# Router worked by halves of the image rows, its vector instructions moved between steps, Newton steps split, round loop written out

## The chip, the cores and the metric

One core of one Trainium2 chip runs the kernel. The metric is the device time of one execution in microseconds; a lower time is better. The engines are named as in the profile: PE is TensorE's matmul, PEld its weight load, DVE is VectorE, ACT ScalarE, POOL GpSimd, SP SyncE (here the only queue that issues DMAs).

## The reference

The input is x[16, 64, 112, 112] in float32. Two blocks are added to it in turn.

```
x = x + conv_ref(ln_c(x))          # ln_c: over the 64 channels of a pixel, eps 1e-6
    pooled = [max over channels, mean over channels]
    conv_ref(v) = v * sigmoid(conv3x3(pooled) + conv_b)
t = tokens of x                    # a token is a pixel, 64 channels
t = t + moe(ln_t(t))               # ln_t: over the channels, eps 1e-5
    router_probs = softmax(v @ router_w + router_b)       # 8 experts
    top 2, their probabilities divided by their sum
    moe(v) = sum over the two of p_k * (v @ expert_w[k] + expert_b[k])
```

## The kernel before

Two images form a pair (`PAIRS` = 8), eight image rows of a pair form a step (`ROWS` = 8, `STEPS` = 14 steps in a pair). Three phases are laid over each other, one pair apart. In round r, phase A reads pair r: PE centres the channels and forms raw router logits (`centre_rows`, L440), ACT copies them out (`centred_to_sbuf`, L877 and L881) and squares them with a running sum (`square`, L896, or `square_group`, L907), and DVE takes the channel maximum (`channel_max`, L639). Phase B of pair r-1 is the router, once a round on tiles of 112 x 224 tokens (all rows of both images): two reciprocal square roots by Newton steps, the 3x3 convolution (`convolve`, L541), its sigmoid, the affine factors, and the choice of the two best experts with ties broken by a priority (`key`, `half_key`, `quarter_key`, `key_max`). Phase C of pair r-2 computes the experts in units: step v has six units for DVE (`scale_unit`, L662: gate from PSUM times x) and two for POOL (L1105, after ACT has copied the gate out, L939). PE spreads the gates (`spread`, L462), multiplies the scaled tokens by the expert weights (`experts`, L517) and adds the biases (`biases`, L511). The eight spreads of a step go through two PSUM slots; one is free again when the unit that read it is done.

The gates come to PE in three bf16 parts made by ACT and POOL (L918, L1113 `rest_one`, L924, L1119 `part_three`), which PE transposes (`turn`, L455) and ACT copies to `s` (`turned_to_sbuf`, L931). The transposes and `centre_rows` write the same PSUM pair `tm`, so that `centre_rows` waits for that copy.

Each engine works through a list written out by hand, the same in each step except for what the router adds. On PE: spread of DVE unit 1 and POOL unit 1, the last experts of v-1, biases, experts 0, `turn`, spreads 2 and 3, `centre_rows` 0, experts 1 and POOL 0, spread 4 and POOL 0 of v+1, (the convolution,) experts 2, `spread_a1`, biases, experts 3, spread 5 and spread 0 of v+1, `centre_rows` 1, experts 4 and POOL 1. DVE: unit 1, `gate(r, step, False)`, the second `finish` of v-1, units 2 and 3, `channel_max`, unit 4, `gate(r, step, True)`, `finish`, unit 5, unit 0 of v+1, `channel_max`. The prediction calls the router's two places in DVE's step the head place and the middle place. POOL: unit 1, `rest_one`, router work, unit 0 of v+1, `scale_x` (L1130), `part_three`.

The router's DVE work before: the whole first square root (11 instructions, L699 to L709) in the middle place of step 0, the second with `rho` in that of step 2; `pooled` in the head of step 1, the affine factors in the head of step 2 (L734 to L741); then one or two instructions in each place, those on `key` with all 224 columns in steps 5, 6, 10 and 11.

Rounds 0 and 1 have no phase C. In round 0 POOL does all squares, after its own setup; ACT may not overwrite a tile before it is squared. Rounds 3 to 7 are a hardware loop (`Fori`) on each engine, with wait counts in registers; the others are written out.

Of the kernel before, what the change touches and what calls it, by code (L numbers as in the profile page):

```python
# [28 lines left out]
ALU = mybir.AluOpType  # L29
# [19 lines left out]
EARLY = 5  # L49
JOIN = 5  # L50
# [14 lines left out]
B_DVE = ("i1", "p1", "t10", "u10", "r10", "t11", "u11", "r11", "t12", "u12", "r1", "pool_max", "pool_mean", "av", "am", "part_sum", "v2", "i2", "p2", "t20", "u20", "r20", "t21", "u21", "r21", "t22", "u22", "r2", "rho",  # L65
         "top_0", "ge_0", "top_1", "ge_1", "key", "half", "quarter", "key_max", "oh1", "dl_0", "dl_1",
         "top2_0", "top2_1", "d", "ge2_0", "ge2_1", "key2", "half2", "quarter2", "key_max2", "oh2")
B_NORM = ("e1", "e2")
GUESS = 0x5F3759DF
B_POOL = ("lg_0", "bias_0", "lg_1", "bias_1", "m1_0", "m1_1", "m2_0", "qb_0", "qg_0", "m2_1", "qb_1", "qg_1")  # L70
B_ACT = ("sig", "wide", "qa_0", "g1", "g2", "wide2", "qa_1")
# [35 lines left out]
def gated_expert_program(nc, x, conv_w, conv_b, router_w, router_b, expert_w, expert_b, const_f, const_g, out):  # L107
# [3 lines left out]
    with ExitStack() as ctx:  # L111
# [131 lines left out]
        def at(r, first, per, n):  # L243
            return (r - first) * per + n if isinstance(r, int) else r * per + (n - first * per)

        def due(count):

            return not isinstance(count, int) or count > 0

        def a_at(r, per_step, step, n):  # L250

            if isinstance(r, int) and r >= PAIRS:
                return PAIRS * STEPS * per_step
# [11 lines left out]
        def on(r, v):  # L265

            return not isinstance(r, int) or 0 <= (r - 2) * STEPS + v < PAIRS * STEPS
# [4 lines left out]
        def squared_at(r, step, n):  # L272

            if isinstance(r, int) and r >= PAIRS:
                return (PAIRS - 1) * STEPS * QUADS
            return at(r, 1, QUADS * STEPS, QUADS * step + n)

        def summed_at(r, step, g):
            if r == 0:
                return NGRP * step + g + 1  # L280
            return NGRP * STEPS + step + 1 + (step // 2 if g == 0 and step % 2 == 0 else (step + 1) // 2 if g == 0 else step // 2 + 1)
# [5 lines left out]
        def centre_pairs(r):  # L287

            early = [moe, gb[:, 0:2, :], gb[:, 2:4, :], tm]
            return [tm] if not isinstance(r, int) or r >= 2 else early[0:4 - r]  # L290
# [34 lines left out]
        prios = prio[:, :].unsqueeze(1).to_broadcast([W, 2 * H, E])  # L325
# [4 lines left out]
        def _(sp):  # L330
# [41 lines left out]
            def body(r, A, steps=STEPS):  # L372
                pairs = [r - n if isinstance(r, int) else sp.snap(r - n) for n in range(4)]
                lead = XA - 1 if isinstance(r, int) and r < 2 else 2
# [907 lines left out]
```

## Time and profile before

| | us |
|---|---|
| median of 3 runs | 1703.19 |
| lowest and highest | 1702.29, 1706.99 |
| profiled execution, its own time | 1706.22 |
| its span, first to last instruction | 1704.4 |

| engine | busy us | share of the span |
|---|---|---|
| PE | 1460.7 | 86% |
| DVE | 1345.4 | 79% |
| POOL | 1142.8 | 67% |
| ACT | 1060.3 | 62% |

The profile is of one execution. The shares are means over a start without phase C (the first 145 us), six rounds with all phases or nearly so, and two rounds without phase A at the end. The granted TensorE clock has a mean of 0.94 of full speed.

### The profile page before, as it was taken

What the parts mean: (1) busy time and instruction counts of PE and PEld (TensorE: products, weight loads), DVE (VectorE), ACT (ScalarE), POOL (GpSimd) and SP (SyncE); (2) the same over time, 40 slices, a digit from 0 to 9 for tenths busy, and PEclk for the clock granted to TensorE, in tenths of its full rate; (3) what the DMA queues carried; (4) which work ended last, traced back from release to release, by engine and by line L of the source; (5) the groups of instructions that cost most, each with busy time, mean ns of one, the idle gap of its engine ahead of it and who ended that gap; (6) DMA issues with size and microseconds to landing.
All of it is one profiled execution on the core that took longest, in us unless ns stands there. A gap on an engine that the chain in (4) does not pass through costs nothing.

```text
span 1704.4 us, 37629 instructions
## 1 busy us (share of the span) xinstructions
PE 1460.7 (86%) x12198; PEld 685.1 (40%) x12198; DVE 1345.4 (79%) x1575; ACT 1060.3 (62%) x4015; POOL 1142.8 (67%) x743
## 2 busy tenths in 40 slices
PE   6865899869997799977999779988799788989999
PEld 5763344434443344433444334433344333323333
DVE  3796888788887788878887788868888778977776
ACT  2566677747776577756777558775678624434442
POOL 6335667848676576855768566775667758788775
PEclk9956899989999999999999899999999989999999
DMA  5441465536555455544655445553555444555554
GB/s 173 120 136 39 120 185 173 174 109 184 176 162 154 141 163 172 164 154 127 183 178 168 126 142 173 175 184 121 151 175 154 129 128 136 171 144 172 174 174 127
DMA packets 85883, 260.40 MB, mean 153 GB/s; under 512 B 13744, under 2 KB 13744, under 8 KB 85680
## 3 DMA queue, kind: packets, MB, share of 16 engines
q1 hardware_dynamic: 85680, 257.85, 50.6%
q8 instruction: 109, 1.79, 0.4%
q14 instruction: 94, 0.77, 0.2%
HBM read 206.41 MB, written 51.38 MB: 151 GB/s over the span
## 4 chain that ended last, share of the span: by engine, by line
PE 54%; DVE 18%; issue 9%; ACT 9%; POOL 1%; DVEq 1%; ACTq 0%; POOLq 0%
PE moe L517 31%; PE gb L462 8%; DVE gx L662 8%; PE tm L440 6%; PE moe L511 4%; ACT s L931 3%; DVE u L704 2%; ACT sq L896 2%; PE tm L501 2%; PE tm L455 2%; DVE quarter_key L771 2%; DVE p L701 2%; DVE u L706 1%; PE tm L541 1%; ACT ge L982 1%
## 5 line engine op out<-in xcount | busy, mean ns | idle before, releaser
L662 DVE TENSOR_TENSOR gx<-gb,xd 128x896 f32<-128x896 f32 x672 | 710.5, 1085 | 205.1 <-PE gb L462 192.2
L517 PE MATMUL moe<-gx,wc 128*64 128x448 f32 x3584 | 841.7, 570 | 1.2 <-POOL parts L1119 1.1
L1105 POOL TENSOR_TENSOR gx<-gs,xd 128x896 f32<-128x896 f32 x224 | 519.0, 2317 | 452.3 <-ACT gs L939 423.6
L939 ACT ACTIVATE gs<-gb 128x896 f32<-128x896 f32 x224 | 204.9, 915 | 302.3 <-PE gb L462 301.7
L462 PE MATMUL gb<-s,cg 54*128 54x448 bf16 x1792 | 273.2, 365 | 118.6 <-DVE gx L662 104.9
L896 ACT ACTIVATE sq<-xct 112x64 f32<-112x64 f32 x1400 | 337.8, 243 | 24.6 <-DVE early_s L649 6.4
L517 PEld LDWEIGHTS moe<-gx,wc 128*64 128x64 f32 x3584 | 221.3, 139 | 247.3 <-issue 190.4
L896 ACT ACTIVATION_READ_ACCUMULATOR sq<-xct 112x1 f32 x1400 | 263.1, 188 | 0.0
L1130 POOL TENSOR_TENSOR tt<-xc,a1s 128x896 f32<-128x896 f32 x112 | 235.2, 2100 | 18.7 <-ACT a1s L946 16.0
L440 PE MATMUL tm<-rhs,xa 64*112 64x74 f32 x2800 | 176.7, 267 | 69.4 <-ACT s L931 63.1
L462 PEld LDWEIGHTS gb<-s,cg 54*128 54x128 bf16 x1792 | 61.1, 95 | 398.9 <-DVE gx L662 229.6
L440 PEld LDWEIGHTS tm<-rhs,xa 64*112 64x112 f32 x2800 | 168.0, 182 | 112.1 <-issue 100.6
L877 ACT ACTIVATE xct<-tm 112x512 f32<-112x512 f32 x175 | 103.9, 594 | 107.9 <-PE tm L440 103.6
L675 DVE TENSOR_TENSOR ot<-moe,tt 128x448 f32<-128x448 f32 x224 | 138.4, 618 | 35.7 <-PE moe L517 35.5
L931 ACT ACTIVATE s<-tm 128x896 bf16<-128x896 bf16 x112 | 102.3, 914 | 80.1 <-PE tm L455 79.8
L946 ACT ACTIVATE a1s<-tm,ones 128x896 f32<-128x896 f32 x112 | 112.8, 1007 | 46.3 <-PE tm L501 46.3
L639 DVE TENSOR_REDUCE stats<-xct 112x8 f32<-112x512 f32 x144 | 97.9, 680 | 41.9 <-ACT logit_mean L881 41.5
L455 PEld LDWEIGHTS tm<-cg,parts 112*64 112x64 bf16 x1792 | 63.8, 115 | 64.0 <-issue 61.4
L1113 POOL TENSOR_TENSOR res<-q,parts 112x288 f32<-112x288 f32 x112 | 87.6, 782 | 0.3 <-ACT parts L918 0.3
L511 PE MATMUL moe<-s,bh 118*64 118x448 bf16 x448 | 84.4, 370 | 0.0
L511 PE MATMUL moe<-s,bl 118*64 118x448 bf16 x448 | 84.1, 369 | 0.0
L1119 POOL TENSOR_TENSOR parts<-res,parts 112x288 bf16<-112x288 f32 x112 | 82.5, 737 | 0.0
(97 smaller groups left out, 1342.5 us busy)
## 6 DMA issues: line engine op xcount, KB each, us to landing
xd<-in_x_dram SPq DMA_DIRECT2D x448, 224.0 KB, 3.9
xa<-in_x_dram SPq DMA_DIRECT2D x112, 448.0 KB, 4.2
xc<-in_x_dram SPq DMA_DIRECT2D x112, 448.0 KB, 4.4
out_dram<-ot SPq DMA_DIRECT2D x112, 448.0 KB, 3.0
gx<-in_const_g_dram SPq DMA_DIRECT2D x1, 384.0 KB, 4.7
cf<-in_const_f_dram SPq DMA_DIRECT2D x1, 332.5 KB, 2.7
gx<-in_L_ffn_expert_w_dram SPq DMA_DIRECT2D x1, 128.0 KB, 4.5
cf<-in_L_ffn_expert_b_dram SPq DMA_DIRECT2D x6, 2.0 KB
```

What stands on the lines that cost most here:

```text
L440: last = pe.matmul(pair[:, b, j, :], xa[chans, step % XA, row * W:(row + 1) * W], rhs1[chans, :], start=True, stop=True)
L462: last = pe.matmul(gb[:, 2 * slot + b, 0:HALF], cg[rows, k * P:(k + 1) * P], s[rows, v % 2, c * HALF:(c + 1) * HALF], start=True, stop=True)
L511: pe.matmul(moe[b * CH:(b + 1) * CH, c, 0:HALF], w[:, b * CH:(b + 1) * CH], s[0:SR, v % 2, c * HALF:(c + 1) * HALF], start=(n == 0), stop= ...
L517: last = pe.matmul(moe[b * CH:(b + 1) * CH, c, 0:HALF], wc[:, k * CH:(k + 1) * CH], gx[:, u, b, :], start=False, stop=(k == KT - 1), skip_ ...
L662: dve.tensor_tensor(gx[:, i, :, :], gb[:, 2 * slot:2 * slot + 2, 0:HALF], xd[:, v % 2, :, c * HALF:(c + 1) * HALF], ALU.mult).then_inc(sca ...
L675: dve.tensor_tensor(ot[:, sl, cols], moe[:, c, 0:HALF], tt[:, sl, cols], ALU.add).then_inc(final, 1)
L896: last = act.activation(sq[:, n, :], xct[:, step % 2, n, :], ACT.Square, accum_out=to[:, 1, lo + n:lo + n + 1])
L931: act.activation(s[:, v % 2, :], turn_out[:, 0:TOK], ACT.Copy).then_inc(s_ready, 1)
L939: act.activation(gs[:, j, :, :], gb[:, 2:4, 0:HALF], ACT.Copy).then_inc(gate_out, 1)
L946: act.activation(a1s[:, v % 2, :].rearrange("p (c t) -> p c t", c=2), tm[:, :, 0:HALF], ACT.Identity, bias=ones[:, :], scale=1.0).then_inc ...
L1105: pool.tensor_tensor(gx[:, ND + j, :, :], gs[:, j, :, :], xd[:, v % 2, :, j * HALF:(j + 1) * HALF], ALU.mult).then_inc(scaled_p, 1)
L1130: pool.tensor_tensor(tt[:, sl, :], xc[:, sl, :], a1s[:, sl, :], ALU.mult).then_inc(scaled_x, 1)
```

## The change

- The router's 224 columns are worked in two halves (`first`, `second`, 112 columns each), one after the other: `half_router(r, h, place)` does eight places for one half. A place is half a step, `place = 2 * step + late`. Half 0 has places 12 to 19, half 1 places 20 to 27. ACT's and POOL's router operations are split and shifted in the same way.
- A Newton root is split: `root_guess` and the first Newton step in one place, the second and the third in the next two. The initial guess is one instruction in place of two.
- On DVE `gate(r, step, False)` stands before unit 1 (was after it), `gate(r, step, True)` before unit 4 (was after it).
- On PE `turn` stands before the biases and experts 0 (was after them); the convolution moves from step 1 to step 2. On ACT `turned_to_sbuf` stands before the last squares of the step before (was after them).
- In round 0, ACT does the squares of the first seven steps (`ACT_STEPS`), POOL those of the others.
- `EARLY` and `JOIN` (how many steps' statistics go to the side tiles, and when they are joined) are 6, were 5.
- Rounds 3 to 7 are written out, with constant wait counts.

```diff
-EARLY = 5
-JOIN = 5
+EARLY = 6
+JOIN = 6
+ACT_STEPS = 7
...
-            with pe.Fori(3, PAIRS) as r:
+            for r in range(3, PAIRS):
                 body(r, True, True)
...
                     if on(r, v - 1):
                         experts_of_dve(r, v - 1, 5)
+                    if ahead:
+                        turn(r, step, v + 1)
                     if cur:
                         biases(r, v, 0)
-                    if ahead:
-                        turn_ready(r, step, v + 1)
-                    if cur:
                         experts_of_dve(r, v, 0)
-                    if ahead:
-                        turn(v + 1)
...
-                    if Bp and step == 1:
+                    if Bp and step == 2:
                         convolve(r, A)
...
+            def largest_key(r, h, again, rows):
+
+                own(r, f"ge{again}_{h}")
+                dve.tensor_tensor(key[:, rows, :], ge[:, rows, :], prios, ALU.mult).then_inc(b_dve, 1)
+                own(r, f"key{again}_{h}")
+                dve.tensor_tensor(half_key[:, rows, :], key[:, rows, 0:4], key[:, rows, 4:8], ALU.max).then_inc(b_dve, 1)
+                own(r, f"half{again}_{h}")
+                dve.tensor_tensor(quarter_key[:, rows, :], half_key[:, rows, 0:2], half_key[:, rows, 2:4], ALU.max) \
+                   .then_inc(b_dve, 1)
+                own(r, f"quarter{again}_{h}")
+                dve.tensor_tensor(key_max[:, rows], quarter_key[:, rows, 0], quarter_key[:, rows, 1], ALU.max) \
+                   .then_inc(b_dve, 1)
...
+            def half_router(r, h, place):
+
+                rows = (first, second)[h]
+                if place == 0:
+                    b_done(dve, r, B_POOL, f"bias_{h}")
+                    largest(top, lg, rows).then_inc(b_dve, 1)
+                elif place == 1:
+                    own(r, f"top_{h}")
+                    at_top(lg, top, rows).then_inc(b_dve, 1)
+                elif place == 2:
+                    largest_key(r, h, "", rows)
+                elif place == 3:
+                    first_expert(r, h)
+                elif place == 4:
+                    second_logit(r, h)
+                elif place == 5:
+                    own(r, f"top2_{h}")
+                    at_top(dl, top2, rows).then_inc(b_dve, 1)
+                elif place == 6:
+                    largest_key(r, h, "2", rows)
+                else:
+                    second_expert(r, h)
...
+                dve.tensor_scalar(p_int, e_int, -0.5, float(GUESS), ALU.mult, ALU.add).then_inc(b_dve, 1)
...
             def gate(r, step, late):
 
...
+                place = 2 * step + late
+                if place == 1:
+                    root_guess(r, 1)
+                    root_step(r, 1, 0, p)
+                elif place == 2:
+                    root_step(r, 1, 1, p)
+                elif place == 3:
+                    root_step(r, 1, 2, r1)
+                elif place == 4:
+                    to_pool(r)
+                elif place == 6:
+                    affine(r)
+                elif place == 7:
+                    root_guess(r, 2)
+                    root_step(r, 2, 0, p)
+                elif place == 8:
+                    root_step(r, 2, 1, p)
+                elif place == 9:
+                    root_step(r, 2, 2, r2)
+                    scale(r)
+                elif 12 <= place < 20:
+                    half_router(r, 0, place - 12)
+                elif place >= 20:
+                    half_router(r, 1, place - 20)
...
-                    if cur:
-                        scale_unit(r, v, 1)
                     if Bp:
                         gate(r, step, False)
+                    if cur:
+                        scale_unit(r, v, 1)
...
-                    if cur:
-                        scale_unit(r, v, 4)
                     if Bp:
                         gate(r, step, True)
                     if cur:
+                        scale_unit(r, v, 4)
                         finish(r, v, 0)
...
                     if parting:
                         part_one(r, v + 2)
+                    if ahead:
+                        turned_to_sbuf(r, v + 1)
+                    if Bp:
+                        router(r, step)
                     if A and step > 0:
                         square(r, step - 1, 3)
...
-            for step in range(STEPS):
+            for step in range(ACT_STEPS, STEPS):
                 for g in range(NGRP):
                     square_group(step, g)
```

POOL's router after: step 0 the first `e` (and the second gates of the round before), step 3 the second `e`, step 5 logits and bias of half 0, steps 6 and 7 those of half 1, steps 9 to 12 the gates of half 0, step 13 and steps 0 to 2 of the next round those of half 1. On ACT `widen` (the widened `key_max`) stands in steps 7, 9, 11 and 13, the sigmoids of the gap in steps 8 and 12.

## Rows read from the trace of the kernel before

**Rows 1.** Windows by round: us, busy (x) of PE, PEld, DVE, ACT, POOL; PEclk, DMA.

```profile
145.70:1369.40 1223.70, 1055.06 (x9074) 482.81 (x9076) 995.45 (x1144) 852.86 (x3548) 830.60 (x505) 0.95 0.52 155
1369.40:1545.20 175.80, 157.53 (x1078) 56.92 (x1080) 141.81 (x149) 66.83 (x92) 133.19 (x82) 0.95 0.50 143
1545.20:1683.40 138.20, 135.78 (x990) 49.58 (x988) 98.90 (x104) 57.16 (x77) 100.39 (x67) 1.00 0.59 174
```

**Rows 2.** Windows: the same columns, steps 1 to 4, 13 and the next 0.

```profile
752.80:771.06 18.26, 17.12 (x121) 8.41 (x122) 12.65 (x14) 10.02 (x41) 9.54 (x6) 0.83 0.43 128
771.06:791.05 19.99, 12.16 (x112) 5.54 (x110) 19.15 (x26) 10.27 (x46) 8.79 (x6) 0.97 0.38 115
791.05:806.56 15.51, 14.37 (x108) 6.15 (x109) 11.03 (x13) 9.54 (x40) 10.68 (x6) 0.82 0.50 152
806.56:819.11 12.55, 11.86 (x110) 5.46 (x109) 10.11 (x12) 9.90 (x44) 11.51 (x8) 1.00 0.62 182
...
924.16:938.86 14.70, 11.93 (x110) 5.42 (x109) 8.90 (x11) 10.26 (x46) 12.36 (x9) 1.00 0.77 240
938.86:958.86 20.00, 13.60 (x109) 6.32 (x110) 15.12 (x20) 10.23 (x43) 10.31 (x7) 0.87 0.34 104
```

**Rows 3.** Timeline of DVE, step 0: start, us, instruction (first root's beginning).

```profile
743.05 2.17 DVE L701 TENSOR_SCALAR p<-p 112x224 int32<-112x224 int32 x1
...
748.27 0.39 DVE L709 SCALAR_TENSOR_TENSOR p<-u,p 112x224 f32<-112x224 f32 x1
```

**Rows 4.** Timeline of POOL beside it.

```profile
742.99 2.09 POOL L1105 TENSOR_TENSOR gx<-gs,xd 128x896 f32<-128x896 f32 x1 [1.40 <-ACT gs L939]
```

**Rows 5.** Timeline of PE: after the burst, and at the convolution.

```profile
752.80 0.56 PE L462 MATMUL gb<-s,cg 54*128 54x448 bf16 x2 [5.70 <-DVE gx L662]
...
763.29 2.52 PE L541 MATMUL tm<-pooled,band 112*112 112x224 f32 x12
```

**Rows 6.** PE, step 13 (head 924.16): biases, turn, spread 2, centring, loop edge; a wait.

```profile
925.44 0.36 PE L511 MATMUL moe<-s,bh 118*64 118x448 bf16 x2
...
926.58 0.57 PE L455 MATMUL tm<-cg,parts 112*64 112x112 bf16 x16
927.08 0.55 PE L462 MATMUL gb<-s,cg 54*128 54x448 bf16 x4
928.33 1.01 PE L440 MATMUL tm<-rhs,xa 64*112 64x74 f32 x16 [0.69 <-ACT s L931]
...
938.86 0.56 PE L462 MATMUL gb<-s,cg 54*128 54x448 bf16 x4 [2.08 <-issue]
...
PE tm L440 <- ACT s L931: 63.1, 82, 1.3
```

**Rows 7.** Timeline of POOL, step 4 (its PE head is at 806.56).

```profile
806.56 0.71 POOL L1119 TENSOR_TENSOR parts<-res,parts 112x288 bf16<-112x288 f32 x1
808.23 2.87 POOL L1105 TENSOR_TENSOR gx<-gs,xd 128x896 f32<-128x896 f32 x1 [0.96 <-ACT gs L939]
```

**Rows 8.** The page's costliest groups: a DVE unit (busy, mean ns, idle before).

```profile
L662 DVE TENSOR_TENSOR gx<-gb,xd 128x896 f32<-128x896 f32 x672 | 710.5, 1085 | 205.1 <-PE gb L462 192.2
```

**Rows 9.** Timeline of DVE: key instructions beside POOL (833), without POOL (104); affine without POOL.

```profile
833.96 2.16 DVE L771 TENSOR_TENSOR quarter_key<-half_key 112x448 bf16<-112x448 bf16 x1
...
104.07 0.61 DVE L769 TENSOR_TENSOR half_key<-key 112x896 bf16<-112x896 bf16 x1
104.72 0.39 DVE L771 TENSOR_TENSOR quarter_key<-half_key 112x448 bf16<-112x448 bf16 x1
...
81.57 0.55 DVE L737 TENSOR_TENSOR avm<-avm,logit_mean 112x224 f32<-112x224 f32 x1
```

**Rows 10.** Start of the kernel: ACT's wait in round 0, first copy of round 1, PE's pace.

```profile
29.48 0.60 ACT L877 ACTIVATE xct<-moe 112x512 f32<-112x512 f32 x1 [16.08 <-POOL sq L1094]
...
62.10 0.60 ACT L877 ACTIVATE xct<-moe 112x512 f32<-112x512 f32 x1 [0.85 <-PE moe L440]
...
14.52 3.19 PE L440 MATMUL gb<-rhs,xa 64*112 64x74 f32 x32
```

More of the change, by code:

```diff
@@ L243, in at @@
         def at(r, first, per, n):
-            return (r - first) * per + n if isinstance(r, int) else r * per + (n - first * per)
+            return (r - first) * per + n
         def due(count):
-            return not isinstance(count, int) or count > 0
+            return count > 0
         def a_at(r, per_step, step, n):
-            if isinstance(r, int) and r >= PAIRS:
+            if r >= PAIRS:
                 return PAIRS * STEPS * per_step
@@ L372, in body @@
             def body(r, A, steps=STEPS):
-                pairs = [r - n if isinstance(r, int) else sp.snap(r - n) for n in range(4)]
-                lead = XA - 1 if isinstance(r, int) and r < 2 else 2
+                pairs = [r - n for n in range(4)]
+                lead = XA - 1 if r < 2 else 2
                 for step in range(steps):
@@ L432, in centre_rows @@
                         pe.wait_ge(a1_out, count)
-                if step == 1 and g == 1 and (not isinstance(r, int) or r >= 2):
+                if step == 2 and g == 1 and r >= 2:
                     b_done(pe, r, B_ACT, "sig")
@@ L614, in _ @@
             body(2, True, True)
-            with pe.Fori(3, PAIRS) as r:
+            for r in range(3, PAIRS):
                 body(r, True, True)
@@ L849, in _ @@
             early_body(0, False)
-            dve.wait_ge(setup_pool, POOL_SETUP)
             early_body(1, True)
             body(2, True, True)
-            with dve.Fori(3, PAIRS) as r:
+            for r in range(3, PAIRS):
                 body(r, True, True)
@@ L871, in centred_to_sbuf @@
                             act.wait_ge(joined, count)
-                    if step == EARLY and (not isinstance(r, int) or r > 0):
-                        b_done(act, r, B_POOL, "lg_1")
+                    if step in (EARLY, STEPS // 2) and r > 0:
+                        b_done(act, r, B_POOL, "lg_0" if step == EARLY else "lg_1")
                 if due(count := a_at(r, NGRP, step, g + 1)):
@@ L976, in affine_to_q, with widen, gates, router @@
                    .then_inc(b_act, 1)
[L978 to L982 removed]
+            def widen(r, h, again):
+                rows = (first, second)[h]
+                b_done(act, r, B_DVE, f"key_max{again}_{h}")
+                act.activation(ge[:, rows, :], wide(key_max, rows), ACT.Copy).then_inc(b_act, 1)
+            def gates(r, h):
+                rows = (first, second)[h]
+                b_done(act, r, B_DVE, f"d_{h}")
+                act.activation(g1[:, rows], gap[:, rows], ACT.Sigmoid, scale=-1.0).then_inc(b_act, 1)
+                act.activation(g2[:, rows], gap[:, rows], ACT.Sigmoid, scale=1.0).then_inc(b_act, 1)
+            def router(r, step):
+                if step == 7:
+                    widen(r, 0, "")
                 elif step == 8:
[L984 removed]
+                    gates(r, 0)
                 elif step == 9:
[L986 to L988 removed]
+                    widen(r, 0, "2")
+                elif step == 11:
+                    widen(r, 1, "")
+                elif step == 12:
+                    gates(r, 1)
+                elif step == 13:
+                    widen(r, 1, "2")
             def early_body(r, Bp):
@@ L1052, in _ @@
             body(2, True, True)
-            with act.Fori(3, PAIRS) as r:
+            for r in range(3, PAIRS):
                 body(r, True, True)
@@ L1253, in _ @@
             body(2, True)
-            with pool.Fori(3, PAIRS) as r:
+            for r in range(3, PAIRS):
                 body(r, True)
```

336 lines of the change are left out of this document (145 added, 191 removed).

## The prediction

> **What bounds the kernel now.** I read the windows first, by round and by step, then the timelines of the dearest steps.
>
> From the first copy of `s` (145.7) six rounds take 1223.7 us, 204.0 each; then a round without phase A takes 175.8, and 13 steps of the last 138.2, or 10.63 a step [rows 1]. Phase A and the router together separate a step of 10.63 from a mean step of 14.6. Step 4 has only two small router instructions and takes 12.55, with PE busy for 11.86 of it at full clock [rows 2]. Fourteen of those are 175.7, so the router costs 28 us a round. Steps 1, 2, 3, 13 and 0 hold nearly all of it: 18.26, 19.99, 15.51, 14.70 and 20.00 [rows 2].
>
> In step 0 DVE starts the root in its middle place. The second instruction takes 2.17, because POOL's unit started 0.06 us earlier: both end near 745.1 [rows 3, 4]. A longer DVE instruction of the same root takes 0.39 [rows 3]. PE, waiting for DVE's unit 5, idles 5.70 us and then continues at half clock: 1.2 GHz shows in the mean clock of 0.83 in step 1 and 0.82 in step 3 [rows 2, 5]. So a burst costs three times: its length, the block by POOL, and the half clock after it.
>
> In ordinary steps PE is the bound with one hole: `centre_rows` waits 0.69 for ACT's `s`, 63.1 us over 82 steps [rows 6].
>
> **Turn earlier.** PE does the first biases and four expert matmuls after `turn` instead of before: `turn` takes the place of the biases at 925.44, 1.1 earlier [rows 6]. The 0.69 hole goes in the steps where nothing else is late. ACT copies `s` before its squares, so it is ready for it. Needed for this is POOL's `part_three`, which ends 0.71 after the head of step 4 [rows 7]; the turn now starts 2.42 after the head and would start 1.3 after it. A step becomes 12.55 - 0.70 = 11.85. The bounds of the gain are 0 (POOL's chain, late by 0.7 in steps with much router work, takes the hole's place) and 63 us. I take 0.70 in steps with phase A. Without phase A there is no such hole, and `part_three` sits later; I charge 0.2 a step there.
>
> **Bursts split.** Nine Newton instructions in a burst become three in a place, about 1.25 us at 0.39 and a gap [rows 3], and two instructions fall away. What a place can hold: in the head place DVE starts at 0.71 (POOL's `part_three` holds it until then), POOL's unit starts at 1.67 [rows 7], and unit 1 must be over when PE wants spread 2, 2.92 after the head (927.08 less 924.16, rows of the turn) [rows 6]. With 1.09 for the unit [rows 8] the head place holds 1.1 us. It also must have *started* its last instruction by 1.67, or it waits for POOL's unit until 3.8. In the middle place, before unit 4, POOL is idle for some 1.7 us, and that is about what fits.
>
> By this, place by place for one round:
> - Newton steps in heads and middles: 0 to 0.2 each. They start at 0.71, 1.13 and 1.55. Cover: PE's experts, turn and biases.
> - Step 0, middle: guess and Newton step wait for POOL's `e`, which follows second gates on POOL. The third instruction meets POOL's unit: +2.4 (between 0, if ahead of it, and 4.2, if two are caught).
> - `pooled`: 0.38 + 0.60, ends at 1.7: 0. The row for the affine multiply without POOL is 0.55 [rows 9]; affine is four instructions of 0.38 to 0.55, and its third would start at 1.70, 0.03 after POOL's unit. I take the block: unit 1 starts at 4.7 in place of 1.75, +2.9 (between 0.2 and 2.9).
> - Four key places, all in heads: multiply 0.61 (half of 1792 columns; 896 take 0.61), half 0.39, quarter and maximum about 0.27 [rows 9]. They start at 0.71, 1.35, 1.77: the quarter is caught, as the full one is now (2.16 against 0.39 alone) [rows 9]. Unit 1 starts at 4.4, PE's spread 2 is 2.5 late: 4 x 2.5 = 10.0 (between 4 x 0.3 and 10.0; the upper end, since a start at 1.77 is after 1.67).
> - Reductions and comparisons with one logit tile (1.1 each), `first_expert` 1.7, ACT's `widen` halves and POOL's operations: they fit their places; lateness of `part_three` and POOL's two operations in step 5, 1.5 together.
> - Convolution: 2.5 on PE as now, only a step later [rows 5].
>
> **The lock, by the notes.** The rows show who starts first: DVE begins beside POOL and waits, or POOL's unit lasts 2.87 when a DVE instruction is in flight [rows 7]. The Trainium skill, SBUF — State Buffer, Who interferes with whom, says that a DVE instruction with two SBUF inputs and a GpSimd instruction that reads SBUF exclude each other for a whole instruction, and that a reduction is exempt. The trace agrees (2.17 and 2.87). That rule speaks against this change: smaller instructions give more starts at which DVE can lose. By it the four key places come to 10 us a round; by a mere sharing of bandwidth they would come to about 1.
>
> **Half clock.** Six places of 2.4 us or more idle PE. Now the loop edge idles it 2.08 [rows 6], and the step after it has a mean clock of 0.87, with the root's idle in it [rows 2]. The pieces of a clock fall are 3.4 us long in the record, so one costs 1.7. I take three a round: 5.1 (0 to 10).
>
> **Rounds written out.** PE waits 2.08 at the loop edge for instructions [rows 6]; four edges, some 8 to 12 us with the clock, go. They are in the 204.0 and not in my base. Written-out rounds already show no such wait.
>
> **Sum of a round.** 14 x 11.85 = 165.9; convolution 2.5; step 0 2.4; affine 2.9; keys 10.0; small 1.5; clock 5.1: 190.3. Less 2.3, because in four steps the 2.5 us idle hides the small items and part of a clock fall: 188. Six rounds: 6 x (204.0 - 188) = 96 us gained. The round without phase A: 148.8 + 2.5 + 2.9 + 10 + 3.4 + 2.8 = 170.4, 5 gained. The last: 13 x 0.2 = 2.6 lost.
>
> **Round 0.** ACT waits 16.08 us for POOL's squares behind its setup [rows 10]. With squares on ACT, the pace is PE's 3.19 for 32 matmuls, 2.99 a step: round 1 starts at 9.5 + 14 x 2.99 = 51.4 in place of 62.1 [rows 10]. ACT and DVE need less for a step. Gain 11 (8 to 12). POOL's setup is over by step 7. Round 1 I leave as it is: DVE's work is a chain with the same instructions, and what the split saves in the burst comes back in the ACT and DVE waits for each other (-6 to +6).
>
> 1704.4 - 96 - 5 + 3 - 11 = 1595 for the span; the profiled run is 1.8 longer than its span, and the median is 3.0 below the profiled run: 1594, say 1595.
>
> **Rivals.**
> - A, the places fit: the keys and the affine factors are not caught, since POOL's unit starts a little later behind a gate copy that waits for its turn on ACT. Then 10 + 2.9 + 3.4 go from each of seven rounds, 16 x 7 = 114: 1480. For it: the two starts are 0.03 and 0.1 us too late only. Against: the gate copy follows the head's spread, which the change leaves alone.
> - B, the turn only changes what it waits for (`part_three`): 0.7 x 84 = 59 comes back: 1654. For it: a unit lengthened to 2.87 [rows 7] puts `part_three` 0.8 later, at 1.5, and the turn is wanted at 1.3.
> - C, slower: each root, key and one-hot place starts after POOL's unit, because ready signals arrive late in a moving schedule. Eight more heads and middles at 2.5, and six more clock falls of 1.7: 30 a round, seven rounds 210: 1805. It decides from some 4.6 further caught places a round on (109 gained / 7 rounds / 3.4 each). Against: Newton steps start at 0.71.
> - D, no change: the router's DVE work only moves and DVE's total is the bound. DVE is busy for 995 of 1224 us, its waits for POOL included [rows 1], 81%, and a round 8% shorter still holds that. About 1700.
>
> **Chances.** Forecast 0.52, A 0.22, B 0.20, C 0.03, D 0.03. The range runs from A to B: 1475 to 1660; C and D and what lies beyond both ends are left out. A measurement of this kernel can tell 0.3% from no change. Faster 0.94, same 0.02, slower 0.04.
>
> **What would show it.** Steps 4, 5, 8 and 10 at 11.9 with no wait of `centre_rows` for `s`: the turn. Quarter and maximum of about 2 us in half the key places, unit 1 late by 2.5: the lock; at 0.3 each, rival A. No PE wait above 4 us after the start. ACT's first copy of round 1 near 51. A wait of the transposes for `part_three` in most steps is B.

## The result and the profile after

| | before | after |
|---|---|---|
| median of 4 runs, us | 1704.61 | 1584.64 |
| lowest and highest | 1702.29, 1706.99 | 1582.87, 1590.98 |
| profiled execution | 1706.22 | 1582.87 |
| its span | 1704.4 | 1581.1 |
| PE, DVE, POOL, ACT busy | 86, 79, 67, 62% | 91, 84, 68, 69% |

The ratio after to before is 0.930, 95% interval 0.927 to 0.933: 120 us faster.

The windows of the kernel after, by round (they answer to [rows 1]) and then for three steps: step 0, the ordinary step 4, and a step with a key place ([rows 2]). Columns: us, busy (x) of PE, PEld, DVE, ACT, POOL; PEclk, DMA share, GB/s.

```profile
137.60:1246.60 1109.00, 1028.29 (x9066) 477.35 (x9068) 965.47 (x1190) 866.01 (x3579) 778.10 (x504) 0.95 0.57 171
1246.60:1420.40 173.80, 154.62 (x1081) 52.96 (x1077) 149.34 (x165) 67.63 (x96) 131.27 (x84) 0.97 0.51 146
1420.40:1558.90 138.50, 135.96 (x991) 46.76 (x988) 98.96 (x105) 57.22 (x77) 102.33 (x68) 1.00 0.59 174
674.87:688.73 13.86, 11.67 (x110) 5.39 (x109) 11.76 (x15) 10.24 (x45) 10.73 (x9) 1.00 0.52 166
726.00:737.60 11.60, 11.60 (x111) 5.37 (x110) 11.41 (x18) 9.92 (x44) 7.64 (x6) 1.00 0.68 200
788.29:804.17 15.88, 13.30 (x110) 5.94 (x108) 13.37 (x16) 10.98 (x46) 9.34 (x8) 0.89 0.50 146
```

The span became 123.3 us shorter. The first copy of `s` comes 8.1 earlier (145.7 to 137.6). The six rounds behind it are 114.7 shorter (1223.7 to 1109.0). The round without phase A is 2.0 shorter, the last 13 steps are 0.3 longer, and what follows them is 1.2 longer.

A round in the middle takes 184.3. Measured between the starts of spread 1, eight of its 14 steps take 11.60 to 11.80; the second window from the end is one of them, with PE busy throughout. The others are step 0 with 13.86, step 2 with 14.06 (11.60 and the convolution's 2.46), and four key steps (7, 9, 11 and 13, whose head place works on `key`) with 15.69 to 15.88.

The last row is the finding: this key step is 4.28 longer than an ordinary one, PE idles for 2.58 of it, and the mean granted clock is 0.89. The four of a round add 16.9. DVE's timeline there, then POOL's and PE's (start, us, instruction, idle time before it):

```profile
788.40 1.05 DVE L692 TENSOR_TENSOR key<-ge,prio 112x896 bf16<-112x896 bf16 x1
789.49 0.39 DVE L694 TENSOR_TENSOR half_key<-key 112x448 bf16<-112x448 bf16 x1
789.92 2.17 DVE L696 TENSOR_TENSOR quarter_key<-half_key 112x224 bf16<-112x224 bf16 x1
792.13 0.67 DVE L699 TENSOR_TENSOR key_max<-quarter_key 112x112 bf16<-112x112 bf16 x1
792.72 1.08 DVE L665 TENSOR_TENSOR gx<-gb,xd 128x896 f32<-128x896 f32 x1
```

```profile
788.27 0.71 POOL L1171 TENSOR_TENSOR parts<-res,parts 112x288 bf16<-112x288 f32 x1
789.88 2.08 POOL L1157 TENSOR_TENSOR gx<-gs,xd 128x896 f32<-128x896 f32 x1 [0.91 <-ACT gs L972]
791.92 0.75 POOL L1165 TENSOR_TENSOR res<-q,parts 112x288 f32<-112x288 f32 x1
```

```profile
793.86 0.55 PE L468 MATMUL gb<-s,cg 54*128 54x448 bf16 x4 [2.58 <-DVE gx L665]
...
795.42 3.03 PE L523 MATMUL moe<-gx,wc 128*64 128x448 f32 x8
```

The quarter maximum starts 0.04 after POOL's unit and lasts 2.17, until POOL's unit is over. The last maximum starts 0.21 after POOL's next operation and takes 0.67, until that one is over. Unit 1 follows at 792.72, 4.43 after the head (788.29), and PE waits for it.

Steps 11 and 13 look the same, with starts 0.03 to 0.04 after POOL's unit. In step 7 POOL's unit starts later (at 763.10, 2.10 after the head), the quarter comes before it and takes 0.27, and the last maximum is the one that is held:

```profile
763.15 2.16 DVE L699 TENSOR_TENSOR key_max<-quarter_key 112x112 bf16<-112x112 bf16 x1
```

The waits of PE and of its weight load, grouped (in total, times, longest). PE's wait for `s` of [rows 6], 63.1 us, is down to 1.3; what PE waits for now are DVE's units. The 37 times are the 28 key places of seven rounds (2.31 to 2.58 each), step 0 with 2.19 to 2.21 in five rounds, and four at the turn to the rounds without phase A:

```profile
PE gb L468 <- DVE gx L665: 91.0, 37, 4.4
...
PE tm L461 <- POOL parts L1171: 3.4, 6, 1.7
...
PEld tm L461 <- POOL parts L1171: 41.4, 97, 2.5
```

### The profile page after: what moved, and what is told of

It is laid out like the page before. It is cut to its first block, busy times and chain, and to the rows that moved or that the text cites. A ratio compares the mean times of both kernels' runs of the same rounds, so it can differ in the third digit from the quotient of the medians.

```text
span 1581.1 us, 34381 instructions
## 1 busy us (share of the span) xinstructions
PE 1432.2 (91%) x12198; PEld 673.0 (43%) x12198; DVE 1326.6 (84%) x1647; ACT 1084.0 (69%) x4061; POOL 1072.8 (68%) x729
## 4 chain that ended last, share of the span: by engine, by line
PE 66%; DVE 16%; issue 8%; ACT 2%; POOL 1%; DVEq 0%; ACTq 0%; POOLq 0%
PE moe L523 36%; PE gb L468 12%; DVE gx L665 8%; PE tm L447 7%; PE moe L517 4%; DVE quarter_key L696 3%; PE tm L507 3%; PE tm L461 2%; DVE key L692 2%; PE tm L547 1%; DVE stats L642 1%; DVE half_key L694 1%; ACT sq L928 1%; ACT logit_mean L994 0%; DVE u L762 0%
## 5 line engine op out<-in xcount | busy, mean ns | idle before, releaser
L1157 POOL TENSOR_TENSOR gx<-gs,xd 128x896 f32<-128x896 f32 x224 | 470.5, 2100 | 400.8 <-ACT gs L972 395.7
L468 PE MATMUL gb<-s,cg 54*128 54x448 bf16 x1792 | 260.3, 359 | 97.0 <-DVE gx L665 91.0
L523 PEld LDWEIGHTS moe<-gx,wc 128*64 128x64 f32 x3584 | 224.8, 140 | 256.2 <-issue 203.6
L1182 POOL TENSOR_TENSOR tt<-xc,a1s 128x896 f32<-128x896 f32 x112 | 236.3, 2110 | 12.5 <-issue 10.7
L468 PEld LDWEIGHTS gb<-s,cg 54*128 54x128 bf16 x1792 | 56.6, 94 | 439.9 <-DVE gx L665 330.4
L447 PEld LDWEIGHTS tm<-rhs,xa 64*112 64x112 f32 x2800 | 182.2, 192 | 29.6 <-issue 11.0
L447 PE MATMUL tm<-rhs,xa 64*112 64x74 f32 x2800 | 180.1, 273 | 11.1 <-ACT logit_mean L913 8.3
L642 DVE TENSOR_REDUCE stats<-xct 112x8 f32<-112x512 f32 x128 | 87.0, 680 | 22.7 <-ACT logit_mean L913 21.6
L1165 POOL TENSOR_TENSOR res<-q,parts 112x288 f32<-112x288 f32 x112 | 81.7, 730 | 9.6 <-ACT parts L951 9.6
L461 PEld LDWEIGHTS tm<-cg,parts 112*64 112x64 bf16 x1792 | 57.2, 111 | 65.4 <-POOL parts L1171 41.4
L517 PE MATMUL moe<-s,bh 118*64 118x448 bf16 x448 | 80.8, 354 | 0.0
L517 PE MATMUL moe<-s,bl 118*64 118x448 bf16 x448 | 80.5, 352 | 0.0
```

What stands on the lines that cost most here:

```text
L447: last = pe.matmul(pair[:, b, j, :], xa[chans, step % XA, row * W:(row + 1) * W], rhs1[chans, :], start=True, stop=True)
L468: last = pe.matmul(gb[:, 2 * slot + b, 0:HALF], cg[rows, k * P:(k + 1) * P], s[rows, v % 2, c * HALF:(c + 1) * HALF], start=True, stop=True)
L517: pe.matmul(moe[b * CH:(b + 1) * CH, c, 0:HALF], w[:, b * CH:(b + 1) * CH], s[0:SR, v % 2, c * HALF:(c + 1) * HALF], start=(n == 0), stop= ...
L523: last = pe.matmul(moe[b * CH:(b + 1) * CH, c, 0:HALF], wc[:, k * CH:(k + 1) * CH], gx[:, u, b, :], start=False, stop=(k == KT - 1), skip_ ...
L1157: pool.tensor_tensor(gx[:, ND + j, :, :], gs[:, j, :, :], xd[:, v % 2, :, j * HALF:(j + 1) * HALF], ALU.mult).then_inc(scaled_p, 1)
L1182: pool.tensor_tensor(tt[:, sl, :], xc[:, sl, :], a1s[:, sl, :], ALU.mult).then_inc(scaled_x, 1)
```

## The experiments

Each kernel is the kernel after with the edit shown, unless it says otherwise. Medians are of 4 runs. "To before" is the ratio to the kernel before on the same chip, with its 95% interval. The kernel before took 1703.75, 1704.33 and 1705.51 in the three groups of runs, so a difference between two groups is uncertain by some 2 us from that alone.

### The key multiply in the place before

```diff
                     at_top(lg, top, rows).then_inc(b_dve, 1)
+                    key_of(r, h, "", rows)      # the same for "2"; largest_key begins with half_key
```

> The changed kernel with one DVE instruction moved: the multiply that makes key goes to the middle place before, behind the comparison (1.08 + 0.61 us there), so that the head place has only half, quarter and maximum, started at about 0.7, 1.1 and 1.4 after the head, ahead of POOL's unit at 1.6. Theory (the instruction that starts after POOL's unit waits for its end, and the clock falls after it): four places of 15.87 us become 11.6 to 11.9, in seven rounds, -28 x 4.2 = -118: some 1470 us. Rival (the chain of four dependent instructions is too long for the place, whatever POOL does, and the sum of DVE's work is moved only): DVE's work is the same, so no change, 1585; or the middle places overflow and the cost moves there, 1560 to 1600.

Measured: 1487.82 us, to before 0.874 (0.872 to 0.875), 97 us faster than the kernel after. DVE's key place, and POOL's unit beside it:

```profile
718.96 0.38 DVE L697 TENSOR_TENSOR half_key<-key 112x448 bf16<-112x448 bf16 x1
719.38 0.28 DVE L699 TENSOR_TENSOR quarter_key<-half_key 112x224 bf16<-112x224 bf16 x1
719.69 0.28 DVE L702 TENSOR_TENSOR key_max<-quarter_key 112x112 bf16<-112x112 bf16 x1
```

```profile
720.30 2.09 POOL L1162 TENSOR_TENSOR gx<-gs,xd 128x896 f32<-128x896 f32 x1 [1.34 <-ACT gs L977]
```

The last maximum ends at 719.97, before POOL's unit starts, and the quarter takes 0.28. The key steps fall from 15.7-15.9 to 11.6, 12.0 and 12.5. TensorE is at half clock for 16.5 us from the start of phase C on, against 98.9 in the kernel after. Most rounds take 170.3 in place of 184.3. That is the 16.9 of the key steps less the 0.9 and 0.4 that two of them keep, and 1.6 for a step 0 that takes 15.2 to 15.5 in three rounds: the same idle of 2.19 us is followed by a fall of the clock there, and was not in the kernel after. These terms, and a round without phase A that becomes only 10.2 shorter, are most of why the gain is 97 and not the 118 expected. The multiply takes 0.62 where it now stands. In the head it took 1.05, started beside `part_three` (788.27 to 788.98 above).

### A reduction for the last two maxima

```diff
-                dve.tensor_tensor(quarter_key[:, rows, :], half_key[:, rows, 0:2], half_key[:, rows, 2:4], ALU.max) \
-                   .then_inc(b_dve, 1)
-                own(r, f"quarter{again}_{h}")
-                dve.tensor_tensor(key_max[:, rows], quarter_key[:, rows, 0], quarter_key[:, rows, 1], ALU.max) \
-                   .then_inc(b_dve, 1)
+                dve.tensor_reduce(key_max[:, rows], half_key[:, rows, :], AX.X, ALU.max).then_inc(b_dve, 1)
```

This leaves the start of the third instruction where it was, and takes only its second input away.

> The changed kernel with one reduction over the four half_key values of a token (one input from SBUF) in place of the two last maxima (two inputs each) in the key places. The chain in the head place is as long: multiply 0.61, half 0.39, reduction about 0.6. Theory (the exclusion between DVE's two-input instructions and POOL's makes the 2.5 us and the clock fall behind them): the reduction starts at 1.8 beside POOL's unit and isn't held; unit 1 starts at 2.4 in place of 4.2, so a key place costs 0.5 to 0.7 in place of 4.27: -28 x 3.7 = -103, some 1482. Rival (a chain of dependent instructions before unit 1 is too long by itself): within 10 us of the changed kernel, 1575 to 1585.

Measured: 1488.09 us, to before 0.873 (0.872 to 0.875), 97 us faster than the kernel after. DVE and POOL in the key place:

```profile
744.70 0.39 DVE L694 TENSOR_TENSOR half_key<-key 112x448 bf16<-112x448 bf16 x1
745.12 0.62 DVE L696 TENSOR_REDUCE key_max<-half_key 112x112 bf16<-112x448 bf16 x1
745.66 1.08 DVE L665 TENSOR_TENSOR gx<-gb,xd 128x896 f32<-128x896 f32 x1
```

```profile
745.09 2.09 POOL L1153 TENSOR_TENSOR gx<-gs,xd 128x896 f32<-128x896 f32 x1 [0.91 <-ACT gs L968]
```

The reduction starts 0.03 after POOL's unit, as the quarter did by 0.04, and takes 0.62. So the place is not too long and POOL does not slow DVE as such: the instruction with two inputs in SBUF, started behind POOL's, waited for its end, and the reduction in its place did not. The Trainium skill, SBUF — State Buffer, Who interferes with whom, exempts a reduction from that exclusion, and these rows agree.

### Both roots in one place each

```diff
                     root_guess(r, 1)
                     root_step(r, 1, 0, p)
-                elif place == 2:
                     root_step(r, 1, 1, p)
-                elif place == 3:
                     root_step(r, 1, 2, r1)
... # and the same for the second root
```

> The changed kernel with both roots again in one place each: guess and three Newton steps in the middle place of step 0 (first root) and of step 3 (second root). Theory (the bursts and what follows them were the largest part of the gain): the fourth instruction meets POOL's unit as now, then seven more at 0.42 us follow, so unit 4 starts 6 us late instead of 2.3, PE idles and its clock falls for 3.4 to 6.8 us: +6 in step 0, +9 in step 3, seven rounds: +90 to +110, about 1680. Rival (the split saved little, and the turn, the loop edges and round 0 made the gain, 22 + 29 + 11 by the runs so far): +50 to +60, 1640.

Measured: 1683.43 us, to before 0.988 (0.986 to 0.989): 98.8 slower than the kernel after. Steps 0 and 3 take 21.1 and 20.0 to 21.0, and PE waits in both:

```profile
734.87 0.93 PE L468 MATMUL gb<-s,cg 54*128 54x448 bf16 x4 [6.91 <-DVE gx L665]
```

The same spread took 0.55 above: the clock has fallen to half. From the start of phase C on it is half for 208 us, against 98.9. Undone alone, the split of the roots is worth more than the turn, round 0 or the written-out rounds; only the placing that comes next is worth more. The bursts stand before unit 4 here, where the kernel before had them behind it, so 98.8 is the price of a burst in the new order.

### DVE's router places behind the units, as before

```diff
-                    if Bp:
-                        gate(r, step, False)
                     if cur:
                         scale_unit(r, v, 1)
+                    if Bp:
+                        gate(r, step, False)   # gate(r, step, True) behind unit 4 likewise
```

> The changed kernel with DVE's router places behind unit 1 and unit 4, as before, all else as changed. Theory (a place must start before POOL's unit starts): head instructions begin at 1.5 after the head, so all but the first are held until 3.7, and in the middle place all are held until POOL's unit ends: +1.5 to +2.5 for most of the 20 places with two-input instructions, in seven rounds: +150 or more, 1735. Rival (the order against the units matters little, since POOL holds DVE only 2.1 us and units 1 and 4 are then in time): within 20 us, 1565 to 1605.

Measured: 1754.17 us, to before 1.029 (1.027 to 1.031): 169.5 slower than the kernel after, and slower than the kernel before. DVE, and POOL beside it:

```profile
800.71 2.33 DVE L790 TENSOR_TENSOR avm<-avm,logit_mean 112x224 f32<-112x224 f32 x1
...
808.64 2.15 DVE L760 TENSOR_TENSOR u<-p 112x224 f32<-112x224 f32 x1
810.82 0.39 DVE L762 SCALAR_TENSOR_TENSOR u<-u,e 112x224 f32<-112x224 f32 x1
811.25 2.16 DVE L765 SCALAR_TENSOR_TENSOR p<-u,p 112x224 f32<-112x224 f32 x1
```

```profile
800.48 2.15 POOL L1158 TENSOR_TENSOR gx<-gs,xd 128x896 f32<-128x896 f32 x1 [1.58 <-ACT gs L973]
...
808.43 2.11 POOL L1158 TENSOR_TENSOR gx<-gs,xd 128x896 f32<-128x896 f32 x1 [3.49 <-ACT gs L973]
```

Behind unit 1 all but the first of the router's instructions start after POOL's unit. In the middle place two of one Newton step are held, the first by POOL's unit and the third by the operation after it. A round takes 211.5. This is the mechanism of rival C. With the other parts kept, the small instructions in their old places cost 169.5, more than the change gained.

### Transposes late on PE

```diff
-                    if ahead:
-                        turn(r, step, v + 1)
                     if cur:
                         biases(r, v, 0)
                         experts_of_dve(r, v, 0)
+                    if ahead:
+                        turn(r, step, v + 1)
```

> The changed kernel with the transposes back behind the biases and experts 0 on PE alone; ACT's order and all else as changed. Theory of the forecast: the hole of 0.69 us before the centring comes back in the 84 steps with phase A, and the step of 11.60 becomes 12.3: +59, 1644. What the changed trace suggests: an ordinary step fell by 0.95, not 0.69, as the matmuls behind a wait also lose their overlap with the ones before: step 12.55, +0.95 x 84 = +80, 1664. Rival: the hole was hidden in the steps with key, where DVE is late anyway: 28 steps less, +53, 1638.

Measured: 1614.15 us, to before 0.948 (0.945 to 0.950): 29.5 slower than the kernel after, half of the 59 of the theory and well under the 53 of the rival. An ordinary step is 12.47 in place of 11.60, about as expected, but step 0 fell from 13.86 to 12.47. Of the key steps one or two a round take 14.1 to 14.3, without a fall of the clock, and another one 17.2 to 17.3, with a fall of twice the length (6.8 us). The four together take 61.5 or 63.0, against 63.3 in the kernel after. What the copy and the centring wait for:

```profile
ACT s L964 <- PE tm L461: 127.5, 111, 1.5
...
PE tm L447 <- ACT s L964: 36.9, 59, 1.3
```

The centring waits in 59 steps, not in 84: the hole and a held place cover each other.

### Both: key multiply early and transposes late

The edits of the first and the last kernel together.

> The kernel with the key multiply one place earlier, and the transposes late on PE. With the key places held by POOL, putting the transposes back cost only 29.5 us, though each ordinary step grew by 0.87. Theory (an idle stretch before the centring and the wait for a late unit 1 or 4 cover each other; where no place is held, the turn's whole gain shows): +0.87 in most of the 84 steps, less the 2.3 of step 0, which the hole covers: +50 to +65 against 1488, 1538 to 1553. Rival (the 29.5 had another cause, such as POOL's chain behind the transposes): again +25 to +35, 1513 to 1523.

Measured: 1538.51 us, to before 0.902 (0.900 to 0.904), 50.7 slower than with the key multiply early alone (48 by the two ratios, since the chips differ). Its step 0 is 12.47 like the others. So the turn is worth some 50 where few places are held and 29.5 where many are.

### The kernel before, rounds written out, and then with the turn

```diff
-            with pe.Fori(3, PAIRS) as r:
+            for r in range(3, PAIRS):          # on each engine
```

> The kernel before with rounds 3 to 7 written out, nothing else changed. Theory: four loop edges, each with a wait of PE for instructions of 2.1 us and sometimes a clock fall of 3.4 us at half speed: -8 to -15, 1690 to 1697. Rival: an edge's wait only takes the place of a later wait for DVE's unit: no change, 1704. Second rival: written-out code makes PE wait for instructions all along: slower.

Measured: 1681.31 us, to before 0.987 (0.985 to 0.989): 22.4 faster, where 8 to 15 were expected. Steps 13 and 0 of it:

```profile
914.42:926.89 12.47, 11.85 (x112) 5.45 (x110) 8.88 (x11) 9.91 (x44) 11.80 (x9) 1.00 0.80 259
926.89:945.04 18.15, 11.92 (x112) 5.46 (x110) 15.41 (x21) 10.42 (x46) 11.03 (x9) 0.92 0.41 127
```

Against the same two in [rows 2] (14.70 and 20.00) that is 2.2 in the one and 1.9 in the other: the idle at the edge, and the half clock that followed it (0.87 in [rows 2], 0.92 here). But [rows 2] show the dearest of the four edges. Another one in the kernel before, and its step 7 in the round of [rows 2]:

```profile
719.45:733.67 14.22, 11.94 (x110) 5.44 (x109) 8.91 (x11) 10.27 (x46) 12.36 (x9) 1.00 0.80 250
733.67:752.80 19.13, 12.29 (x108) 5.64 (x108) 15.21 (x20) 10.11 (x43) 10.32 (x7) 0.98 0.34 107
845.14:859.93 14.79, 13.49 (x110) 5.67 (x109) 11.01 (x13) 10.93 (x50) 8.02 (x6) 0.88 0.49 155
```

PE idles 2.08 at the edge of [rows 2] and 1.50 to 1.62 at the other three, and only the first is followed by a fall of the clock. By steps 13 and 0 together the four edges cost 2.7, 2.7, 4.1 and 2.4, which is 11.9. The other half of the 22.4 lies away from the edges. Each of the five rounds of the loop has one fall of the clock in step 7 or 12, which takes 14.8 where all written-out rounds take 13.1, and the ordinary steps are 12.55 where written-out ones are 12.47. Why the looped rounds differ inside was not tested.

The same kernel with the turn early on PE and ACT:

> The kernel before with the rounds written out and the transposes earlier on PE and their copy earlier on ACT; the router as before. Theory: an ordinary step falls from 12.55 to 11.60, so against the written-out kernel alone up to 84 x 0.95 = -80: some 1615 to 1630 us. Rival: in the kernel before POOL's part_three ends later (its unit is lengthened by DVE instructions in flight), so the transposes wait for it and the gain is 0.4 to 0.6 a step: -35 to -50, 1645 to 1660.

Measured: 1653.37 us, to before 0.971 (0.969 to 0.973), 27.9 faster than the one above it. The rival was nearer: its range of times holds, though the gain is less than its 35 to 50. What the transposes wait for:

```profile
PEld tm L455 <- POOL parts L1118: 63.8, 93, 2.6
...
PE tm L455 <- POOL parts L1118: 11.7, 12, 2.4
```

The two rows are the weight load's wait and the matmul's. In the kernel after, the weight load still waits 41.4 in 97 places, but PE only 3.4 in 6, and the ordinary step is 11.60 there, where it is 11.7 to 12.2 here. So on its own the turn partly changes what it waits for, as rival B said. With the router's work in its new places that wait costs PE almost nothing.

### Squares of round 0 all on POOL

```diff
-ACT_STEPS = 7
+ACT_STEPS = 0
```

The edit also leaves out POOL's wait for a sum in step 0, where no step is before it.

> The changed kernel with all squares of round 0 on POOL again. Theory: ACT waits for POOL's setup as in the kernel before, round 1 starts at 62 in place of 51, and nothing of it is made good later: +11, 1595. Rival: round 1 is held by the same chain of DVE and ACT and begins to be so later, so that part of the 11 is hidden: +4 to +7.

Measured: 1595.69 us, to before 0.935 (0.933 to 0.937): 11.1 slower, as expected, or 8 by the two ratios. In the trace spread 1 of the first step with phase C starts 10.6 later (156.32 for 145.77), which speaks for the 11. ACT waits for POOL's squares again:

```profile
29.48 0.60 ACT L909 ACTIVATE xct<-moe 112x512 f32<-112x512 f32 x1 [16.13 <-POOL sq L1147]
```

### Better versions: the first root shifted, and over four places

Both stand on the kernel with the key multiply early. The first moves the Newton steps' last product on by one place, so that the middle place of step 0 has three instructions, but that of step 1 has four:

```diff
-                    root_step(r, 1, 0, p)
+                    root_open(r, 1, 0)
                 elif place == 2:
-                    root_step(r, 1, 1, p)
+                    root_close(r, 1, 0, p)
+                    root_open(r, 1, 1)
                 elif place == 3:
+                    root_close(r, 1, 1, p)
                     root_step(r, 1, 2, r1)
```

> The changed kernel with the key multiply one place earlier, as in the run that did that alone, and the first root's products shifted: guess and two products in the middle of step 0, then one left over and two, then one left over and three. Theory: the instruction of step 0 that POOL's unit holds for 2.15 us is gone from there, step 0 falls from 13.86 to about 11.8, with the clock falls behind it in some rounds: -19 against 1488, about 1469. Rival (the four instructions in the next head or middle place are held in its stead): no change against 1488.

Measured: 1489.69 us, to before 0.874 (0.872 to 0.876), no gain. Step 0 became 11.67, but step 1 rose from 11.6 to between 13.8 and 15.4. DVE in its middle place, and POOL:

```profile
650.18 0.86 DVE L778 SCALAR_TENSOR_TENSOR p<-u,p 112x224 f32<-112x224 f32 x1
...
651.93 2.16 DVE L778 SCALAR_TENSOR_TENSOR r<-u,p 112x224 f32<-112x224 f32 x1
```

```profile
648.69 2.11 POOL L1240 TENSOR_TENSOR q<-lg,dl 112x896 f32<-112x896 f32 x1
651.71 2.12 POOL L1172 TENSOR_TENSOR gx<-gs,xd 128x896 f32<-128x896 f32 x1 [0.92 <-ACT gs L987]
```

The fourth starts 0.22 after POOL's unit. The second version puts it into a fourth place, the head of step 2. Against the first version:

```diff
                     root_close(r, 1, 1, p)
-                    root_step(r, 1, 2, r1)
+                    root_open(r, 1, 2)
                 elif place == 4:
+                    root_close(r, 1, 2, r1)
                     to_pool(r)
```

> The changed kernel with the key multiply one place earlier and the first root over four places of three instructions (guess and two; one and two; one and two; then one with the two that write pooled). Theory: in the run that left four instructions to the middle of step 1, the fourth was held by POOL's unit there (15.3 us for that step in place of 11.6). With three in each place no instruction starts after POOL's unit: steps 0 and 1 take 11.6 to 11.7 each, the head of step 2 is full but in time: -2.2 x 7 and three or four clock falls of 1.7 less: -20, about 1468. Rival: the third of the head of step 2 is held in its stead: no change against 1488.

Measured: 1468.96 us, to before 0.861 (0.859 to 0.863), 18.9 faster than with the key multiply early alone and the fastest kernel here: 236 us under the kernel before, almost twice the gain of the change. Its six rounds, and steps 0 and 1:

```profile
145.81:1154.43 1008.62, 996.04 (x9081) 461.48 (x9079) 910.25 (x1193) 855.79 (x3552) 791.45 (x506) 0.99 0.63 189
...
627.73:639.40 11.67, 11.65 (x112) 5.36 (x110) 9.59 (x14) 10.07 (x45) 9.88 (x7) 1.00 0.63 199
639.40:651.00 11.60, 11.60 (x112) 5.38 (x110) 11.46 (x17) 9.95 (x44) 9.84 (x7) 1.00 0.67 200
```

PE is busy for 996 of 1009 us at a clock of 0.99, so PE's own list is now the bound.

## Why the prediction was right, and where its terms were off

The forecast was 1595, the median is 1584.64. The mechanism that it gave the largest chance is the one in the trace. The nearness is partly luck: the ordinary step and the affine factors came out cheaper than forecast, the clock and round 1 dearer. In the table us are counted, and what gains is shorter.

| term | predicted | in the trace |
|---|---|---|
| ordinary step | 11.85 | 11.60 |
| convolution, step 0 | 2.5, 2.4 | 2.46, 2.26 |
| affine factors | 2.9 | 0 |
| four key places, with the clock | 10.0 + 5.1 | 16.9 |
| small items, less cover | 1.5 - 2.3 | 0.2 |
| a round | 188 | 184.3 |
| round without phase A | gains 5 | gains 2.0, or 3.1 by the starts of spread 1 |
| round 0 | gains 11 | 11.1 |
| round 1 | as it was | loses 3.7 |
| four loop edges | 8 to 12 | 11.9, of 22.4 for written-out rounds (on the kernel before) |
| last steps | lose 2.6 | lose 0.3 |

**Turn.** An ordinary step is 0.87 shorter with the turn early (11.60 against 12.47), where I took the hole's 0.70. PE in step 3 after:

```profile
717.31 0.55 PE L468 MATMUL gb<-s,cg 54*128 54x448 bf16 x4
717.70 0.92 PE L447 MATMUL tm<-rhs,xa 64*112 64x74 f32 x16
```

From the spread to the centring is 0.39, where it was 1.25 in [rows 6]. So without the wait of 0.69 the centring starts 0.16 before the recorded end of the spread, and with it 0.70 behind that end: the wait also cost the overlap of the two. The other 0.08 from the 12.55 of [rows 2] goes with the written-out rounds, which have 12.47. But 59 us for 84 steps was too much: undone alone the turn gives back 29.5, with the key places free 50.7. That sum took every step for an ordinary one, where steps with a held place hide the hole.

**Affine factors.** I had the third instruction 0.03 too late, and named that margin. DVE, and POOL's unit:

```profile
714.50 0.38 DVE L787 SCALAR_TENSOR_TENSOR avm<-sig,r 112x224 f32<-112x224 f32 x1
...
715.83 0.39 DVE L794 SCALAR_TENSOR_TENSOR top<-avm,gap 112x224 f32<-112x224 f32 x1
```

```profile
713.67 0.74 POOL L1171 TENSOR_TENSOR parts<-res,parts 112x288 bf16<-112x288 f32 x1
...
715.98 2.19 POOL L1157 TENSOR_TENSOR gx<-gs,xd 128x896 f32<-128x896 f32 x1 [1.57 <-ACT gs L972]
```

The convolution keeps PE for 2.46 in the step before, so that POOL is through with `part_three` at 714.41, when PE's head comes at 714.39. DVE starts 0.11 after the head and not 0.71, and the fourth instruction starts 0.15 before POOL's unit. A margin of 0.1 cannot be decided from a trace in which the step before was another one. That the convolution is the cause is read from this trace; no run moved it back.

**Keys and the clock.** The block came in all four places of every round, and its price of 2.5 was right (2.38 to 2.58). In step 7 it caught the last maximum, not the quarter. The falls of the clock were four in five of the six rounds, where I took three. The mean of 0.89 over 15.88 us is 3.5 us at half clock, so one costs 1.7. The round without phase A lost the same places. By the starts of spread 1 it fell from 173.1 to 170.0, the 170.4 of the sum; I had compared that with the 175.8 of a window with other ends.

**What is held.** Of the two numbers that I set beside the rule on two SBUF inputs, the 2.17 of [rows 3] is an int32 instruction with one SBUF input, so it says nothing of two inputs; the row that does is the 2.16 of [rows 9]. The 2.17 shows that one input alone does not make an instruction free. The reduction was free, in its own run.

**Loop edges.** I priced four idles of 2.08 with the clock at 8 to 12. The edges cost 11.9: one with 2.08 and a fall of the clock behind it, three with 1.50 to 1.62 and none. I had attributed all of the 0.87 of the step behind the edge to the root. What I had at nothing is the other half of the 22.4, the falls of the clock in step 7 or 12 and the 0.08 a step inside the looped rounds.

**Step 0.** As forecast, one instruction was held (the predicted one, the last of the Newton step):

```profile
682.63 2.15 DVE L765 SCALAR_TENSOR_TENSOR p<-u,p 112x224 f32<-112x224 f32 x1
```

**Round 0** came as forecast: ACT's first copy of round 1 is at 50.98 in place of 62.10 [rows 10]. Round 1 took 81.3 from there to ACT's first copy of round 2, 77.6 before, inside the bounds of -6 to +6 but on the dear side. No experiment was made on that.

**Where the parts went.** Measured one at a time, the written-out rounds give 22.4, the turn 29.5, round 0 11.1, the split of the roots 98.8: 162 in all, against 120 for the change. The steps show where the rest is given back. In the round of [rows 2], steps 0 to 3 took 73.2 (with 17.69 for the step 1 that belongs to that step 0), and 51.1 after: 22.1 gained. Steps 4 to 13 took 132.3, and 133.1 after. In these ten steps the turn was worth 8.7 (ten times 0.87) and the edge 2.2, and the key steps took all of it back, since the halves made four held places with a half clock behind each, where the full-width keys had made steps of 13.2 to 14.8. For six rounds and four edges that is some 60 us by estimate, more than the missing 42; the parts do not add up exactly, as the two prices of the turn show. The placing before the units (169.5) is not in this sum, because the other parts stand on it. `EARLY` and `JOIN`, the convolution's step, ACT's place for the copy of `s` and the shorter guess were not undone alone.

**Rivals.** Of A (1480) only the affine part happened, but its price was right: with the key places free as well the kernel takes 1488. B is wrong for the change as a whole, and half right for the turn alone. C is what happens without the new places: 1754, where I had 1805. D falls with DVE at 84% and the round 10% shorter.

## What to carry to other kernels

Where POOL reads SBUF and DVE has instructions with two SBUF inputs beside it, count such an instruction by when it starts, not by how long it is: put it ahead of POOL's next start, move the longest piece to an earlier place, or turn it into a reduction. A hold costs what the bound engine then waits, and the clock behind it: here 2.58 became 4.28. Price parts that share a step together: a wait removed beside another wait is worth less than alone, 29.5 against some 50 here.

## What the runs showed of the hardware beyond the forecast

- Behind 25 of the 28 idles of PE in the key places (2.31 to 2.58 us) the clock fell to 1.2 GHz, for 3.4 us each time, and so it did behind the 2.08 at one loop edge. The 2.19 in step 0 was not followed by a fall in the kernel after, but the same 2.19 was in three of five rounds with the key multiply early, and nine of 24 idles of 2.38 to 2.59 with the transposes late were not. So the length of the idle alone does not tell. In the key step above eight expert matmuls take 3.03 at the lower clock, and the eight that end the step take 1.72 at 2.4 GHz.
- An edge of the hardware loop cost this kernel 2.4 to 4.1 us, 11.9 for four, with PE idle for 1.50 to 2.08 of each. The Trainium skill, Advanced Engine Details and Errata, Control Flow Timing, gives about 108 ns for a compare-and-branch. The measurement decides: what an edge costs is far more than the branch.
- A reduction of 0.62 us, with one input, ran freely beside a POOL operation of 2.09 us, where an instruction of 0.28 us with two inputs took 2.17. An int32 instruction with one input was held all the same, for 2.17 [rows 3].
